# Attention loop on one Trainium2 core: VectorE's rotation moved behind the maxima of each step, and the maxima's turning product widened to 128 columns

## The chip, the cores and the metric

One Trainium2 chip; the kernel runs on one of its cores. The metric is device time in microseconds (us) of one execution. Engines are named as the profile names them: PE is TensorE's matmul, PEld its weight load, DVE VectorE, ACT ScalarE, POOL GpSimd, SP the queue that issues transfers. L543 is line 543 of the kernel before.

## The reference, cut to what matters

The model has four layers over 2048 rows of 128 features; the change touches the first alone, a full attention with 16 heads of 64:

```python
qkv = x @ qkv_w + qkv_b                      # heads H=16, D=64
q, k = rope(q), rope(k)                      # (t0*cos - t1*sin, t1*cos + t0*sin) on even/odd pairs
attn = softmax(einsum('bhqd,bhkd->bhqk', q, k) / 8)
out = einsum('bhqk,bhkd->bhqd', attn, v)
y = out @ out_w + out_b
```

Three more layers follow (a local attention with its feed-forward part, a scan, a gated feed-forward part), each with a layer norm.

## The kernel before

`mha_heads` computes the attention. Numbers go through TensorE as pairs of float16 (a high part and the remainder, "lo"), so that products keep float32-like precision. The work is cut into 64 **turns** (16 heads by 4 chunks of 512 queries), each of 8 **steps**; a step takes 256 of the 2048 keys. There are 512 steps, and each engine has the loop over them written out by hand; semaphores join the engines. I write j for the step within a turn, e for the turn.

In step p (turn e, step j) the engines do this:

- **PE**: `scores(p)`, four products of 512 columns (L385, L386) into `p_s`; `maxima`, two products of 512 columns (L370), one for each half of `p_m`, for the step 12 ahead (LEAD_M); `weigh`, twice twelve products of 64 or 65 columns (L400, L402, L404) for the step three back (LAG), into `p_o`. The order in a step is scores, first maxima product, 12 of weigh, second maxima product, 12 of weigh; at j=2 the first twelve and the first maxima product stand ahead of the scores. Added to this, once in each turn: at j=0 three projection products of 512 columns for the turn six ahead (L330 to L332, into `p_a`), at j=6 `turn_max` (L375, one product, which turns the negated maxima of 128 partitions x 4 into rows of `p_a`), at j=7 `project_v` (twelve products of 64 columns).
- **ACT**: two exponentials of each score block, to `probs_hi` in float16 (L511) and `probs` in float32 (L514); at j=4 also `high` (L474), the float16 copy of the rotated q and k.
- **POOL**: `probs_lo` = `probs` - `probs_hi` (L306), one instruction in each step; once in every four turns, after j=3, `split_weights` for a later head (L266, L268).
- **DVE**: two maxima reductions in each step (L589), one for each half of `p_m`. A product of `maxima` waits until the reduction of the step before has emptied the same half. Around the reductions stand, once in each turn: `cross_sin` (L543), `cross_cos` (L549), `cross_first` (L554) and `cross_second` (L558), the rotation of q and k; `low` (L569), the float16 remainder; `normalise` (L610, L612); `negate_max` (L596); `max_rows` (L602), which reads what `turn_max` wrote; `high_v` and `low_v` (L574, L579).
- **SP**: twelve transfers in each turn that spread `hi` and `lo` to the tiles of q and k.

`turn_max(e+1)` waits for `negate_max` (m_done) and for `low` (lo_done), since it writes the bank that `low` reads. `project_v` waits for `max_rows`, and the projection of the next turn for `low_v`. `weigh(p)` waits for POOL's `lo_pool`, `scores(p)` for the exponentials of step p-2. The projection, rotation, `low` and `project_v` are made for the turn six ahead, so the last six turns don't have them; the loop's transfers run far ahead of their use.

Of the kernel before, what the change touches and what calls it, by code (L numbers as in the profile page):

```python
# [6 lines left out]
ALU = mybir.AluOpType  # L7
ACT = mybir.ActivationFunctionType
AX = mybir.AxisListType.X
F32 = mybir.dt.float32  # L10
F16 = mybir.dt.float16
I32 = mybir.dt.int32

P = 128
# [5 lines left out]
TPC = CH // P  # L20
# [84 lines left out]
TURNS = HEADS * QC  # L105
STEPS_A = TURNS * PAIRS_A


LAG = 3
# [3 lines left out]
LEAD_M = 12  # L113
# [9 lines left out]
def phase_mha(nc, x_sb, ident, a, ln, local_scope, late_scope):  # L123


    with Scope(nc, "a_") as sc:
        attn = sc.sb("attn", [P, NT, HEADS * HD])
        wo = sc.sb("wo", [P, HEADS * HD // P, D])
        mha_heads(nc, x_sb, ident, a, attn, wo)
        late = LateWeights(late_scope, a)  # L130
        local = LocalWeights(local_scope, late_scope, a)
        mha_out(nc, x_sb, ident, ln, attn, wo, local, late)
    return local, late


def chunk(c):
    return slice(c * CH, (c + 1) * CH)


def mha_heads(nc, x_sb, ident, a, attn, wo):  # L140

    IC = HEADS * HD // P
    with Scope(nc, "ah_") as sc:
# [15 lines left out]
        hi = sc.sb("hi", [P, 2, CH], F16)  # L159
        lo = sc.sb("lo", [P, 2, CH], F16)  # L160
        part = sc.sb("part_max", [P, TPC, 4])
        negm = sc.sb("neg_max", [P, TPC], F16)
        identh = sc.sb("ident_f16", [P, P], F16)
        pb = sc.sb("probs", [P, RP, 2, CH])
        ph = sc.sb("probs_hi", [P, RW, 2, CH], F16)
# [9 lines left out]
        p_a = sc.ps("p_a", [P, CH])  # L175
# [13 lines left out]
        LAST_G = TURNS - 1  # L189
# [21 lines left out]
        with nc.Block() as block:  # L211
# [100 lines left out]
            def _(pe):  # L312
                pe.wait_ge(ident_in, 16)
                for c in range(NCH):
# [3 lines left out]
                    for t in range(TPC):  # L318
                        mm = pe.transpose(p_m[:, c % 2, t * P:(t + 1) * P], x_sb[:, c * TPC + t, :], ident[:, :])
                    mm.then_inc(x_turned, 1)  # L320
                pe.wait_ge(consts, 1)

                def project(out, g, which, ready):
                    h, c = divmod(g, QC)
# [47 lines left out]

                def turn_max(e):
                    pe.wait_ge(m_done, e + 1)
                    pe.matmul(p_a[0:TPC, 0:P], negm[:, :], identh[:, :], start=True, stop=True).then_inc(m_turned, 1)  # L375

                def scores(p):
                    e, j = divmod(p, PAIRS_A)
# [35 lines left out]
                for c in range(IC):  # L414
                    mm = pe.matmul(p_a[:, 0:D], bv[:, c:c + 1].to_broadcast([P, P]), wo[:, c, :], start=(c == 0),
                                   stop=(c == IC - 1))
                mm.then_inc(bias_turned, 1)
                early_v(LEAD_G - 2)
                for q in range(PAIRS_A):
                    maxima(q)  # L420
                pe.wait_ge(bias_done, 1)
                turn_max(0)
                early_v(LEAD_G - 1)
                for q in range(PAIRS_A, LEAD_M):
# [5 lines left out]
                for p in range(STEPS_A):  # L430
                    e, j = divmod(p, PAIRS_A)
                    g = e + LEAD_G
# [87 lines left out]
            def _(dve):  # L520
# [16 lines left out]
                def cross_sin(g):  # L537
                    h = g // QC
                    dve.wait_ge(proj_ready, g + 1)
                    dve.wait_ge(r_done, g)  # L540
                    if g > LEAD_G:
                        dve.wait_ge(first_half, g - LEAD_G)
                    dve.scalar_tensor_tensor(rot[:, :], p_a[:, :], bqk[:, 2, h:h + 1], sin[:, chunk(g % QC)], ALU.add,  # L543
                                             ALU.mult).then_inc(rot_done, 1)

                def cross_cos(g):
                    h = g // QC
                    dve.wait_ge(rot_done, g + 1)
                    dve.scalar_tensor_tensor(p_a[:, :], p_a[:, :], bqk[:, 2, h:h + 1], cos[:, chunk(g % QC)], ALU.add,  # L549
                                             ALU.mult).then_inc(cos_done, 1)  # L550

                def cross_first(g):
                    dve.wait_ge(cos_done, g + 1)
                    dve.tensor_tensor(p_a[0:HD, :], p_a[0:HD, :], rot[HD:P, :], ALU.add).then_inc(first_half, 1)  # L554

                def cross_second(g):
                    dve.wait_ge(cos_done, g + 1)
                    dve.tensor_tensor(p_a[HD:P, :], p_a[HD:P, :], rot[0:HD, :], ALU.subtract).then_inc(r_done, 1)  # L558
# [6 lines left out]
                def low(g):  # L565
                    dve.wait_ge(hi_done, g + 1)
                    if g >= 2:
                        dve.wait_ge(spread[g % 2], spread_after(g // 2))
                    dve.tensor_tensor(lo[:, g % 2, :], proj_bank(g), hi[:, g % 2, :], ALU.subtract).then_inc(lo_done, 1)  # L569

                def high_v(g):
                    h, c = divmod(g, QC)
                    dve.wait_ge(v_ready, g + 1)
                    dve.tensor_copy(vh[:, h % SETS, c * TPC:(c + 1) * TPC, 0:HD], v_tiles(g)).then_inc(vh_done, 1)  # L574

                def low_v(g):
                    h, c = divmod(g, QC)
                    dve.wait_ge(vh_done, g + 1)
                    dve.tensor_tensor(vl[:, h % SETS, c * TPC:(c + 1) * TPC, :], v_tiles(g),  # L579
                                      vh[:, h % SETS, c * TPC:(c + 1) * TPC, 0:HD], ALU.subtract).then_inc(vl_done, 1)  # L580

                def reduce_max(q, halves=(0, 1)):
                    e, i = divmod(q, PAIRS_A)
                    t, half = divmod(i, 2)
                    if i == 0 and e >= 1 and 0 in halves:
                        dve.wait_ge(m_done, e)
                    for b in halves:
                        dve.wait_ge(m_ready, 2 * q + b + 1)
                        dve.tensor_reduce(part[:, t, 2 * half + b:2 * half + b + 1], p_m[:, b, :], AX,  # L589
                                          ALU.max).then_inc(maxed, 1)  # L590

                def negate_max(e):
                    dve.wait_ge(maxed, 2 * PAIRS_A * (e + 1))
                    if e >= 1:
                        dve.wait_ge(m_turned, e)
                    dve.tensor_reduce(negm[:, :], part[:, :, :], AX, ALU.max, negate=True).then_inc(m_done, 1)  # L596

                def max_rows(e):
                    n, c = divmod(e, QC)
                    dve.wait_ge(m_turned, e + 1)  # L600
                    rows = qb[0:TPC, n % SETS, chunk(c)].rearrange("r (t q) -> r t q", q=P)
                    dve.scalar_tensor_tensor(rows, p_a[0:TPC, 0:P].unsqueeze(1).to_broadcast([TPC, TPC, P]), EXP_SHIFT,  # L602
                                             ident[0:TPC, 0:TPC].unsqueeze(2).to_broadcast([TPC, TPC, P]), ALU.add,
                                             ALU.mult).then_inc(mrow_ready, 1)

                def normalise(e):
                    n, c = divmod(e, QC)
                    dve.wait_ge(o_ready, e + 1)
                    o = p_o[:, 0:TPC * VW].rearrange("p (t w) -> p t w", w=VW)
                    dve.reciprocal(rcp[:, :], o[:, :, HD]).then_inc(rcp_done, 1)  # L610
                    dve.wait_ge(rcp_done, e + 1)
                    dve.tensor_tensor(attn[:, c * TPC:(c + 1) * TPC, n * HD:(n + 1) * HD], o[:, :, 0:HD],  # L612
                                      rcp[:, :].unsqueeze(2).to_broadcast([P, TPC, HD]), ALU.mult).then_inc(o_free, 1)

                dve.wait_ge(ident_in, 16)
                dve.tensor_copy(identh[:, :], ident[:, :]).then_inc(consts, 1)
                for c in range(NCH):
                    dve.wait_ge(xh_ready, c + 1)
                    dve.tensor_tensor(xl[:, chunk(c)], p_m[:, c % 2, :], xh[:, chunk(c)],
                                      ALU.subtract).then_inc(xl_ready, 1)  # L620
# [21 lines left out]
                for p in range(STEPS_A):  # L642
                    e, j = divmod(p, PAIRS_A)
                    g = e + LEAD_G
                    if p + LEAD_M < STEPS_A:
                        reduce_max(p + LEAD_M, (0,))
                    if g <= LAST_G:
                        if j == 1:
                            cross_cos(g)
                        if j == 3:  # L650
                            cross_second(g)
                        if j == 5:
                            low(g)
                    if j == LAG - 1 and e >= 1:
                        normalise(e - 1)
                    if p + LEAD_M < STEPS_A:
                        reduce_max(p + LEAD_M, (1,))
                    if j == 3 and e + 1 < TURNS:
                        negate_max(e + 1)
                    if g <= LAST_G:  # L660
                        if j == 0:
                            cross_sin(g)
                        if j == 2:
                            cross_first(g)
                        if j == 7:
                            high_v(g)
                            low_v(g)
                    if j == 6 and e + 1 < TURNS:
                        max_rows(e + 1)
                normalise(TURNS - 1)  # L670


# [1734 lines left out]
```

## Time and profile before

| | |
|---|---|
| time, median of 3 runs | 1828.27 us (1826.53 to 1828.4) |
| profiled execution, its own time | 1826.56 us |
| its span (first to last instruction) | 1824.8 us |
| PE busy | 1701.7 us (93%) |
| DVE busy | 1462.3 us (80%) |
| ACT busy | 1429.3 us (78%) |
| POOL busy | 1427.8 us (78%) |
| mean granted clock of TensorE | 0.978 of full speed |

Busy times are unions of an engine's instructions; a 512-column product has 0.38 us in the records though the next one starts 0.215 us later, so PE's busy share hides small gaps, and start times are read instead. The attention loop runs from 56.6 us to about 1195 us; the granted clock is 1.00 from 60 us to the end of the loop.

### The profile page before, as it was taken

How to read it: one execution, taken by the hardware profiler on the slowest of the kernel's cores; microseconds unless marked ns; L12 is line 12 of the kernel's file. 1: busy time of each engine (PE TensorE's matmuls, PEld its weight loads, DVE VectorE, ACT ScalarE, POOL GpSimd, SP SyncE). 2: the span in 40 equal slices, each digit the busy share in tenths (PEclk: the TensorE clock that was granted, in tenths of full speed). 3: DMA queues.
4: the chain of work that ended last, by engine and by line, in shares of the span. 5: the costliest groups of instructions: out<-in, count | busy, mean ns of one | idle time of the engine just before them, and what ended most of it. 6: DMA issues, size and time to landing. Idle time of an engine off the chain costs nothing. (4 is left out here: it accounts for less than half of the span.)

```text
span 1824.8 us, 53957 instructions
## 1 busy us (share of the span) xinstructions
PE 1701.7 (93%) x22682; PEld 1080.8 (59%) x22682; DVE 1462.3 (80%) x2658; ACT 1429.3 (78%) x1795; POOL 1427.8 (78%) x851
## 2 busy tenths in 40 slices
PE   5999999999999999999999999986989999978997
PEld 2466666666666666666666666683556666653454
DVE  5888888888888888888888887445988888855785
ACT  2688888888888888888888889834898888853464
POOL 6799999999999999999999999973665566624122
PEclk9899999999999999999999999997999999989999
DMA  5001010101001010100101010050211111110000
GB/s 143 21 25 28 22 30 22 27 25 27 24 25 26 24 31 20 29 24 25 26 25 27 20 28 2 2 169 17 44 38 37 37 37 37 34 26 1 1 0 24
DMA packets 76648, 56.12 MB, mean 31 GB/s; under 512 B 34764, under 2 KB 69752, under 8 KB 76408
## 3 DMA queue, kind: packets, MB, share of 16 engines
q1 hardware_dynamic: 76408, 52.69, 11.2%
q8 instruction: 179, 2.93, 0.7%
q14 instruction: 61, 0.50, 0.1%
HBM read 13.76 MB, written 1.05 MB: 8 GB/s over the span
## 5 line engine op out<-in xcount | busy, mean ns | idle before, releaser
L306 POOL TENSOR_TENSOR ah_probs_lo<-ah_probs,ah_probs_hi 128x1024 f16<-128x1024 f32 x512 | 1074.3, 2134 | 60.0 <-ACT ah_probs L514 60.0
L589 DVE TENSOR_REDUCE ah_part_max<-ah_p_m 128x1 f32<-128x512 f32 x1024 | 673.2, 685 | 140.7 <-PE ah_p_m L370 128.4
L511 ACT ACTIVATE ah_probs_hi<-ah_p_s 128x1024 f16<-128x1024 f32 x512 | 538.2, 1051 | 146.2 <-PE ah_p_s L386 139.9
L514 ACT ACTIVATE ah_probs<-ah_p_s 128x1024 f32<-128x1024 f32 x512 | 540.6, 1056 | 0.0
L400 PE MATMUL ah_p_o<-ah_v_hi,ah_probs_hi 128*128 128x65 f16 x4096 | 470.1, 195 | 5.7 <-POOL ah_probs_lo L306 5.1
L402 PE MATMUL ah_p_o<-ah_v_lo,ah_probs_hi 128*128 128x64 f16 x4096 | 470.3, 193 | 0.0
L404 PE MATMUL ah_p_o<-ah_v_hi,ah_probs_lo 128*128 128x65 f16 x4096 | 470.1, 194 | 0.0
L402 PEld LDWEIGHTS ah_p_o<-ah_v_lo,ah_probs_hi 128*128 128x128 f16 x4096 | 378.0, 98 | 96.9
L400 PEld LDWEIGHTS ah_p_o<-ah_v_hi,ah_probs_hi 128*128 128x128 f16 x4096 | 383.1, 98 | 71.9 <-POOL ah_probs_lo L306 8.8
L370 PE MATMUL ah_p_m<-ah_k_hi_lo,ah_q_hi_twice 128*128 128x512 f16 x1024 | 393.8, 385 | 21.4 <-DVE ah_part_max L589 18.0
L385 PE MATMUL ah_p_s<-ah_q_hi_twice,ah_k_hi_lo 128*128 128x512 f16 x1024 | 388.9, 380 | 0.8 <-ACT ah_probs L514 0.4
L386 PE MATMUL ah_p_s<-ah_max_q_lo,ah_one_k_hi 128*128 128x512 f16 x1024 | 388.3, 379 | 0.0
L404 PEld LDWEIGHTS ah_p_o<-ah_v_hi,ah_probs_lo 128*128 128x128 f16 x4096 | 379.2, 97 | 0.0
L370 PEld LDWEIGHTS ah_p_m<-ah_k_hi_lo,ah_q_hi_twice 128*128 128x128 f16 x1024 | 100.1, 98 | 99.2 <-DVE ah_part_max L589 36.4
L385 PEld LDWEIGHTS ah_p_s<-ah_q_hi_twice,ah_k_hi_lo 128*128 128x128 f16 x1024 | 100.0, 98 | 70.3 <-ACT ah_probs L514 1.4
L386 PEld LDWEIGHTS ah_p_s<-ah_max_q_lo,ah_one_k_hi 128*128 128x128 f16 x1024 | 100.1, 98 | 68.6 <-issue 0.3
L1079 POOL TENSOR_TENSOR ba_rot_sum<-ba_rot_parts 128x512 f32<-128x512 f32 x64 | 80.2, 1273 | 61.6 <-DVE ba_rot_parts L1464 61.6
L1102 POOL TENSOR_TENSOR ba_qk<-ba_rot_sum,ba_rnorm 128x1024 f32<-128x1024 f32 x32 | 60.9, 1903 | 72.5 <-issue 71.8
L1464 DVE TENSOR_TENSOR ba_rot_parts<-ba_p_qk,bw_rot 128x1024 f32<-128x1024 f32 x64 | 75.5, 1217 | 33.4 <-ACT ba_sq L1365 33.0
L1094 POOL TENSOR_TENSOR ba_probs_lo<-ba_probs,ba_probs_hi 128x1024 f16<-128x1024 f32 x32 | 68.2, 2131 | 5.6 <-ACT ba_probs L1374 5.6
L1365 ACT ACTIVATE ba_sq<-ba_p_qk 128x512 f32<-128x512 f32 x64 | 37.4, 593 | 39.6 <-PE ba_p_qk L1119 38.5
L2050 POOL TENSOR_TENSOR t_o_norm<-t_centred,t_rstd 128x512 f32<-128x512 f32 x4 | 4.3, 1076 | 69.3 <-DVE t_rstd L2142 69.3
(317 smaller groups left out, 3085.9 us busy)
## 6 DMA issues: line engine op xcount, KB each, us to landing
ba_v_skew<-ba_v_own SPq DMA_DIRECT2D x64, 129.0 KB, 2.3
ah_q_hi_twice<-ah_hi SPq DMA_DIRECT2D x232, 32.0 KB, 1.9
ah_k_hi_lo<-ah_hi SPq DMA_DIRECT2D x116, 32.0 KB, 1.9
ah_one_k_hi<-ah_hi SPq DMA_DIRECT2D x116, 32.0 KB, 1.9
ah_k_hi_lo<-ah_lo SPq DMA_DIRECT2D x116, 32.0 KB, 1.9
ah_max_q_lo<-ah_lo SPq DMA_DIRECT2D x116, 32.0 KB, 1.9
bw_rot<-in_rot SPq DMA_DIRECT2D x4, 512.0 KB, 9.8
ao_wqkv<-in_wqkv SPq DMA_DIRECT2D x2, 768.0 KB, 6.9
```

Of the source, the lines that this page charges most:

```text
L306: pool.tensor_tensor(pl[:, p % RW, :, :], pb[:, p % RP, :, :], ph[:, p % RW, :, :], ALU.subtract).then_inc(lo_pool, 1)
L370: pe.matmul(p_m[:, b, :], qa[:, s, rows], ka[:, s, chunk(2 * half + b)], start=True, stop=True).then_inc(m_ready, 1)
L385: pe.matmul(p_s[:, p % 2, i, :], ka[:, s, ks], qa[:, s, chunk(c)], start=True, stop=False)
L386: mm = pe.matmul(p_s[:, p % 2, i, :], kb[:, s, ks], qb[:, s, chunk(c)], start=False, stop=True)
L400: pe.matmul(o, hi_i, vh[:, s, kt, :], start=(kt == 0 and i == 0), stop=False, skip_group_check=True)
L402: pe.matmul(o[:, 0:HD], hi_i, vl[:, s, kt, :], start=False, stop=False, skip_group_check=True)
L404: mm = pe.matmul(o, lo_i, vh[:, s, kt, :], start=False, stop=(kt == KT - 1), skip_group_check=True)
L511: act.activation(ph[:, p % RW, :, :], p_s[:, p % 2, :, :], ACT.Exp, scale=HD ** -0.5)
L514: act.activation(pb[:, p % RP, :, :], p_s[:, p % 2, :, :], ACT.Exp, scale=HD ** -0.5).then_inc(exp_done, 1)
L589: dve.tensor_reduce(part[:, t, 2 * half + b:2 * half + b + 1], p_m[:, b, :], AX, ALU.max).then_inc(maxed, 1)
L1079: pool.tensor_tensor(out[:, :, :, f, :], part[:, :, 0, :, f, :], part[:, :, 1, :, 1 - f, :], ALU.add).then_inc(t3_done, 1)
L1464: dve.tensor_tensor(t12[:, s, :, :].rearrange("p r (h d) -> p r h d", d=DH), x4.unsqueeze(1).to_broadcast([P, 2, HEADS_B, DH]), lw.tab[:, ...
```

## The change

Two things are changed.

1. VectorE's order. Before, at odd steps (`cross_cos` j=1, `cross_second` j=3, `low` j=5) one operation of the rotation stood between the two reductions of a step. Now every one stands behind the second reduction, and `cross_cos` follows `cross_sin` at j=0. `negate_max` (j=3) comes after `cross_second`. `max_rows` (j=6) moves the other way, from behind the second reduction to between the two; `normalise` (j=2) stays between them.
2. `turn_max`. The tile of negated maxima is widened from 4 to 128 columns; columns 4 to 127 are set to zero once, at the start, and the product uses all 128 as its weights and writes 128 rows of `p_a` in place of 4. The first four are read as before.

```diff
-        negm = sc.sb("neg_max", [P, TPC], F16)
+        negm = sc.sb("neg_max", [P, P], F16)
...
-                pe.wait_ge(consts, 1)
+                pe.wait_ge(consts, 2)
...
-                    pe.matmul(p_a[0:TPC, 0:P], negm[:, :], identh[:, :], start=True, stop=True).then_inc(m_turned, 1)
+                    pe.matmul(p_a[:, 0:P], negm[:, :], identh[:, :], start=True, stop=True).then_inc(m_turned, 1)
...
-                    dve.tensor_reduce(negm[:, :], part[:, :, :], AX, ALU.max, negate=True).then_inc(m_done, 1)
+                    dve.tensor_reduce(negm[:, 0:TPC], part[:, :, :], AX, ALU.max, negate=True).then_inc(m_done, 1)
...
+                dve.memset(negm[:, TPC:P], 0.0).then_inc(consts, 1)
...
                     if p + LEAD_M < STEPS_A:
                         reduce_max(p + LEAD_M, (0,))
+                    if j == LAG - 1 and e >= 1:
+                        normalise(e - 1)
+                    if j == 6 and e + 1 < TURNS:
+                        max_rows(e + 1)
+                    if p + LEAD_M < STEPS_A:
+                        reduce_max(p + LEAD_M, (1,))
                     if g <= LAST_G:
-                        if j == 1:
+                        if j == 0:
+                            cross_sin(g)
                             cross_cos(g)
+                        if j == 2:
+                            cross_first(g)
                         if j == 3:
                             cross_second(g)
                         if j == 5:
                             low(g)
-                    if j == LAG - 1 and e >= 1:
-                        normalise(e - 1)
-                    if p + LEAD_M < STEPS_A:
-                        reduce_max(p + LEAD_M, (1,))
-                    if j == 3 and e + 1 < TURNS:
-                        negate_max(e + 1)
-                    if g <= LAST_G:
-                        if j == 0:
-                            cross_sin(g)
-                        if j == 2:
-                            cross_first(g)
                         if j == 7:
                             high_v(g)
                             low_v(g)
-                    if j == 6 and e + 1 < TURNS:
-                        max_rows(e + 1)
+                    if j == 3 and e + 1 < TURNS:
+                        negate_max(e + 1)
```

The order of VectorE's instructions in one turn (the second of the loop), from `cross_sin` at j=0 to `negate_max` at j=3, before:

```order
L543 SCALAR_TENSOR_TENSOR ah_rot_sin<-ah_p_a,ah_bias_qk,ah_sin 128x512
L589 TENSOR_REDUCE ah_part_max<-ah_p_m 128x1
L549 SCALAR_TENSOR_TENSOR ah_p_a<-ah_p_a,ah_bias_qk,ah_cos 128x512
L589 TENSOR_REDUCE ah_part_max<-ah_p_m 128x1 x2
L610 RECIPROCAL ah_rcp<-ah_p_o 128x4
L612 TENSOR_TENSOR a_attn<-ah_p_o,ah_rcp 128x4x64
L589 TENSOR_REDUCE ah_part_max<-ah_p_m 128x1
L554 TENSOR_TENSOR ah_p_a<-ah_p_a,ah_rot_sin 64x512
L589 TENSOR_REDUCE ah_part_max<-ah_p_m 128x1
L558 TENSOR_TENSOR ah_p_a<-ah_p_a,ah_rot_sin 64x512
L589 TENSOR_REDUCE ah_part_max<-ah_p_m 128x1
L596 TENSOR_REDUCE ah_neg_max<-ah_part_max 128x4
```

The same place in the changed kernel:

```order
L543 SCALAR_TENSOR_TENSOR ah_rot_sin<-ah_p_a,ah_bias_qk,ah_sin 128x512
L549 SCALAR_TENSOR_TENSOR ah_p_a<-ah_p_a,ah_bias_qk,ah_cos 128x512
L589 TENSOR_REDUCE ah_part_max<-ah_p_m 128x1 x3
L610 RECIPROCAL ah_rcp<-ah_p_o 128x4
L612 TENSOR_TENSOR a_attn<-ah_p_o,ah_rcp 128x4x64
L589 TENSOR_REDUCE ah_part_max<-ah_p_m 128x1
L554 TENSOR_TENSOR ah_p_a<-ah_p_a,ah_rot_sin 64x512
L589 TENSOR_REDUCE ah_part_max<-ah_p_m 128x1 x2
L558 TENSOR_TENSOR ah_p_a<-ah_p_a,ah_rot_sin 64x512
L596 TENSOR_REDUCE ah_neg_max<-ah_part_max 128x4
```

L549 has gone ahead of the reductions of j=1, and L558 behind the second reduction of j=3. The rest of the same turn, j=4 to j=7, in the changed kernel:

```order
L589 TENSOR_REDUCE ah_part_max<-ah_p_m 128x1 x4
L569 TENSOR_TENSOR ah_lo<-ah_p_a,ah_hi 128x512
L589 TENSOR_REDUCE ah_part_max<-ah_p_m 128x1
L602 SCALAR_TENSOR_TENSOR ah_max_q_lo<-ah_p_a,g_ident 4x512
L589 TENSOR_REDUCE ah_part_max<-ah_p_m 128x1 x3
L574 CAST ah_v_hi<-ah_p_a 128x4x64
L579 TENSOR_TENSOR ah_v_lo<-ah_p_a,ah_v_hi 128x256
```

Before, L569 stood one reduction earlier and L602 one reduction later. On PE the order stays; at j=6 the turning product alone has another form:

```order
 L370 MATMUL ah_p_m<-ah_k_hi_lo,ah_q_hi_twice 128x512
-L375 MATMUL ah_p_a<-ah_ident_f,ah_neg_max 4x128
+L375 MATMUL ah_p_a<-ah_ident_f,ah_neg_max 128x128
 L400 MATMUL ah_p_o<-ah_v_hi,ah_probs_hi 128x65
```

It stands where it stood, between the second maxima product of j=6 and the twelve products of `weigh`.

## Rows read from the trace of the kernel before

**Rows 1.** Waits, 99.39 to 1098.23 us: engine, line, waited for, us, times, longest

```profile
PE ah_p_m L370 <- DVE ah_part_max L589: 14.4, 56, 0.3
PEld ah_p_a L375 <- issue: 13.4, 56, 0.2
```

**Rows 2.** Timeline of PE, one turn's bounds, first score product at j=0

```profile
608.26 0.38 PE L385 MATMUL ah_p_s<-ah_q_hi_twice,ah_k_hi_lo 128*128 128x512 f16 x1
...
626.11 0.38 PE L385 MATMUL ah_p_s<-ah_q_hi_twice,ah_k_hi_lo 128*128 128x512 f16 x1
```

**Rows 3.** Timeline of PE at j=4: the two maxima products, weigh between them

```profile
617.85 0.38 PE L370 MATMUL ah_p_m<-ah_k_hi_lo,ah_q_hi_twice 128*128 128x512 f16 x1
618.07 0.19 PE L400 MATMUL ah_p_o<-ah_v_hi,ah_probs_hi 128*128 128x65 f16 x1
...
618.40 0.19 PE L404 MATMUL ah_p_o<-ah_v_hi,ah_probs_lo 128*128 128x65 f16 x1
618.85 0.39 PE L370 MATMUL ah_p_m<-ah_k_hi_lo,ah_q_hi_twice 128*128 128x512 f16 x1 [0.26 <-DVE ah_part_max L589]
```

**Rows 4.** Timeline of DVE, the same turn: start, duration, instruction, idle before

```profile
610.77 0.75 DVE L543 SCALAR_TENSOR_TENSOR ah_rot_sin<-ah_p_a,ah_bias_qk,ah_sin 128x512 f32<-128x512 f32 x1
...
612.93 0.76 DVE L549 SCALAR_TENSOR_TENSOR ah_p_a<-ah_p_a,ah_bias_qk,ah_cos 128x512 f32<-128x512 f32 x1
...
616.05 0.69 DVE L554 TENSOR_TENSOR ah_p_a<-ah_p_a,ah_rot_sin 64x512 f32<-64x512 f32 x1
616.66 0.67 DVE L589 TENSOR_REDUCE ah_part_max<-ah_p_m 128x1 f32<-128x512 f32 x1
617.36 0.71 DVE L558 TENSOR_TENSOR ah_p_a<-ah_p_a,ah_rot_sin 64x512 f32<-64x512 f32 x1
618.10 0.69 DVE L589 TENSOR_REDUCE ah_part_max<-ah_p_m 128x1 f32<-128x512 f32 x1
618.83 0.17 DVE L596 TENSOR_REDUCE ah_neg_max<-ah_part_max 128x4 f16<-128x16 f32 x1
...
620.72 0.69 DVE L589 TENSOR_REDUCE ah_part_max<-ah_p_m 128x1 f32<-128x512 f32 x1 [0.40 <-PE ah_p_m L370]
...
623.94 0.67 DVE L602 SCALAR_TENSOR_TENSOR ah_max_q_lo<-ah_p_a,g_ident 4x512 f16<-4x512 f32 x1
```

**Rows 5.** Timeline of PE, the first maxima product at j=5

```profile
620.30 0.38 PE L370 MATMUL ah_p_m<-ah_k_hi_lo,ah_q_hi_twice 128*128 128x512 f16 x1
```

**Rows 6.** Timeline of PE around the turning product at j=6

```profile
622.54 0.19 PE L400 MATMUL ah_p_o<-ah_v_hi,ah_probs_hi 128*128 128x65 f16 x1
...
622.90 0.38 PE L370 MATMUL ah_p_m<-ah_k_hi_lo,ah_q_hi_twice 128*128 128x512 f16 x1
623.21 0.22 PE L375 MATMUL ah_p_a<-ah_ident_f,ah_neg_max 128*4 128x128 f16 x1
623.36 0.20 PE L400 MATMUL ah_p_o<-ah_v_hi,ah_probs_hi 128*128 128x65 f16 x1
```

**Rows 7.** Groups by line, 80 to 1180 us: busy, mean ns, idle before

```profile
L370 PEld LDWEIGHTS ah_p_m<-ah_k_hi_lo,ah_q_hi_twice 128*128 128x128 f16 x978 | 95.6, 98 | 79.3 <-DVE ah_part_max L589 21.5
...
L375 PEld LDWEIGHTS ah_p_a<-ah_ident_f,ah_neg_max 128*4 128x4 f16 x62 | 5.0, 80 | 14.6 <-issue 14.6
```

**Rows 8.** Timeline of POOL: a plain turn, one with split_weights, the last turns

```profile
616.96 14.66 POOL L306 TENSOR_TENSOR ah_probs_lo<-ah_probs,ah_probs_hi 128x1024 f16<-128x1024 f32 x7 [0.83 <-ACT ah_probs L514]
...
652.66 4.22 POOL L306 TENSOR_TENSOR ah_probs_lo<-ah_probs,ah_probs_hi 128x1024 f16<-128x1024 f32 x2 [0.83 <-ACT ah_probs L514]
...
657.76 12.58 POOL L306 TENSOR_TENSOR ah_probs_lo<-ah_probs,ah_probs_hi 128x1024 f16<-128x1024 f32 x6
...
1081.03 16.77 POOL L306 TENSOR_TENSOR ah_probs_lo<-ah_probs,ah_probs_hi 128x1024 f16<-128x1024 f32 x8 [0.83 <-ACT ah_probs L514]
1098.23 96.12 POOL L306 TENSOR_TENSOR ah_probs_lo<-ah_probs,ah_probs_hi 128x1024 f16<-128x1024 f32 x46 [0.43 <-ACT ah_probs L514]
```

**Rows 9.** Timeline of ACT, the float16 copy of the rotated q and k

```profile
620.38 0.66 ACT L474 ACTIVATE ah_hi<-ah_p_a 128x512 f16<-128x512 f32 x1
```

## The prediction

> **What bounds the kernel now.** I read the granted clock first (1.00 all through the attention loop, so no term here hangs on it), then the waits in the steady loop, then the timelines of PE, DVE and POOL over one turn. The change touches only the loop of 512 steps. In it a turn lasts 626.11 - 608.26 = 17.85 us [rows 2], the same in every turn that I looked at. PE's products stand back to back nearly everywhere: a 512-column product takes 0.215 us of PE's time (617.85 to 618.07, [rows 3]), the twelve of `weigh` or of `project_v` 0.365 (622.54 to 622.90, [rows 6]). A turn has 51 of the first (32 scores, 16 maxima, 3 projections) and 17 of the second: 10.97 + 6.20 = 17.17 us. So about 0.65 us of each turn is not dense work, and it lies in two places.
>
> First, at j=4 PE has ended `weigh` at 618.07 + 0.365 = 618.43 but starts the second maxima product at 618.85: **0.42 us lost** [rows 3]. It waits for the half that j=3's second reduction empties, and that reduction (618.10 to 618.79) stood behind `cross_second`, 617.36 to 618.07 [rows 4]. PE starts 0.06 us after it ends. The waits show the same stop in each turn, 56 times in 56 turns; their 14.4 us are smaller than 56 x 0.42, because the recorded ends of `weigh`'s products cover part of the gap [rows 1]. The waits, then, undercount; starts don't.
>
> Second, around the turning product at j=6: the maxima product starts at 622.90, the turning product at 623.21, `weigh` at 623.36 [rows 6]. Dense, these would be 0.215 and, for 128 columns, 0.215 x 128/512 = 0.054. Measured 0.31 + 0.15 = 0.46 against 0.27: **0.19 us lost**. The load of 4 columns is not pulled ahead as the other loads are ("issue", 0.2 us, 56 times, [rows 1]), with nothing outstanding: `negate_max` ended at 619.00, `low` before 622.
>
> 0.42 + 0.19 = 0.61, and 17.85 - 0.61 = 17.24 agrees with 17.17 + 0.054. PE would be dense at 17.24 us.
>
> POOL is next. Seven of its instructions take 14.66 us [rows 8]; one lasts 2.13, so the pitch is 12.53/6 = 2.09 and a turn needs 16.71 us. A turn with `split_weights` needs 657.76 - 652.66 - 2 x 2.09 = 0.92 more [rows 8]. In the last 46 steps (no projections, no rotation) POOL is the bound: 96.12 us with no gap [rows 8]. Nothing of the change shortens these.
>
> **The change, part by part.** I count PE's time T from the first score product of a turn. With dense PE the maxima products start at T = 0.86, 1.44 (j=0), 3.53, 4.11 (j=1), 5.05, 6.49 (j=2), 7.57, 8.14 (j=3), 9.59, 10.17 (j=4), 11.61, 12.19 (j=5), 13.63, 14.21 (j=6), 15.71, 16.29 (j=7). A reduction can start 0.42 us after its product (620.30 to 620.72, [rows 5, 4]) and takes 0.69.
>
> *Sine and cosine back to back (j=0).* The last projection product starts at T 2.09, so sine runs 2.51 to 3.26, cosine 3.30 to 4.06 (durations 0.75 and 0.76, [rows 4]). j=1's first reduction, ready at 3.95, runs 4.1 to 4.8; PE wants it done for 5.05. Hidden by 0.25.
>
> *Rotation behind the second reduction (j=2, j=3).* j=2's second reduction runs 6.91 to 7.60, `cross_first` to 8.32 (0.69), j=3's reductions to 9.03 and 9.74, `cross_second` to 10.47 (0.71), `negate_max` to 10.66, j=4's reductions to 11.37 and 12.08. This counts durations end to end; the rows let a reduction start up to 0.08 before its predecessor's recorded end (616.66 against 616.05 + 0.69), so it is cautious. PE wants j=3's second at 10.17 (0.43 to spare, where before it came 0.42 late) and j=4's two at 11.61 and 12.19 (0.24 and 0.11 to spare). So the **0.42 us goes, and what is late next is nothing on DVE**: the three operations fit in the time of the four score products. `high` on ACT ran at 620.38, T = 12.1 [rows 9], long after `cross_second` even at its new end 10.47, so it is not delayed, nor are the transfers on SP that follow it.
>
> *`low` (j=5)* now ends about T 14.0 (j=5's second reduction starts 12.65, then 0.69 and 0.68); `turn_max` wants it at 14.43. Its four transfers leave some 0.7 us later, on data wanted a whole turn later.
>
> *`max_rows` between the reductions (j=6).* This adds a wait: in DVE's queue j=6's second reduction now stands behind `max_rows`, and that behind PE's turning product. The product starts at T 14.43; 0.22 (its record, [rows 6]) and 0.04 later DVE can go: 14.69 to 15.36 (0.67, [rows 4]), the reduction to 16.05. PE wants it at 16.29. Hidden by 0.2; DVE's idle time costs nothing. `project_v` waits less for `max_rows` than before.
>
> *128 columns.* The 0.19 us goes, if the width of the load is what holds it back. The price may lie anywhere from 0.27 us for the pair of products (all gained) to 0.46 (nothing gained); I take 0.27, since 128-column loads stand before every other product and none shows the gap. The load itself lasts 98 ns against 80 [rows 7], beside a running product. By the Trainium skill ("TensorE: Matmul & The Clock Gate", LDWEIGHTS) a load costs its columns divided by 1.2 per ns, an estimated 3 ns for 4 columns and 107 for 128; were that serial, the product would gain only 0.09 us a turn, and the sum would be 5.9 us worse. The row's 80 ns for 4 columns speaks against it. The memset at the start is one instruction of DVE, taken as nothing, since PE waits for later work of DVE.
>
> *POOL.* In plain turns its idle time shrinks from 17.85 - 16.71 = 1.14 to 0.53 us. In a `split_weights` turn it needs 17.63 against 17.24. Before, `weigh` of j=7, made by PE at j=2 of the next turn, starts at T 4.69, here 608.26 + 4.69 = 612.95. POOL began j=2 of the turn before at 616.96 - 17.85 = 599.11 [rows 8] and ended j=7 at 599.11 + 5 x 2.09 + 2.13 = 611.69, 1.26 us earlier. Now 1.26 - 0.61 - 0.92 = -0.27, and with 0.06 of release PE waits **0.33 us in each of the 14 such turns**: 4.7 us given back.
>
> *Sum.* Turn 0 has its own shape (less `weigh`, DVE busy throughout); I give it 0.4 of gain. Turns 1 to 56: 56 x 0.61 = 34.2. At the end POOL's queue takes over: it idles 0.43 us before its last 46 steps [rows 8], and that goes too, instead of 0.61 for turn 57. 0.4 + 34.2 + 0.4 - 4.7 = **30.3 us**. The profiled execution took 1826.56 us (span 1824.8 and 1.8 around it): 1796.3. The median of the runs shown lies 1.7 above it: 1798.0. I say 1797.
>
> **The rivals.** (A) The forecast above.
>
> (B) Only the product gains; the stop moves along DVE's queue instead of leaving (to j=1, where cosine ends 0.25 before it matters, or to j=4 and j=5, where 0.11 is left). Then 57 x 0.19 = 10.8 us, nothing given back by POOL: 1816. For it: spare times are small. Against it: four separate places have to be off by several tenths, and my durations are cautious.
>
> (C) Only the order gains: the 0.19 belongs to the product's waits on semaphores, not to its width. 57 x 0.42 = 23.9, POOL gives back 14 x 0.15: 1805. Against it: the projections wait for semaphores as well and leave no gap. The Trainium skill ("TensorEngine Tiling (Array Packing)", Key Properties) says that changing the tiling mode drains TensorE; by that, 4 columns are the cause and C is wrong, and the `128*4` in the product's row [rows 6] is such a mode.
>
> (D) Slower: `max_rows` holds up j=6's second reduction, so PE stops at j=7's second maxima product, the wait that takes the place of the one removed. It decides once the turned row reaches DVE more than 0.24 us after T 14.69, and the kernel is slower than before only from 0.24 + 0.61 = 0.85 on. At 1.0 us late: 57 x 0.15 = 8.6 more than 1827, 1836. It would take `low` ending beyond T 15.3, against 14.0.
>
> (E) The gain is met by POOL more harshly than I count: its plain turns run late too, and PE waits in each. With 16.71 + 0.92/4 = 16.94 us a turn on average it can't take back more than the 4.7 plus some coupling; twice that gives 1802. It lies in A's own range.
>
> **How the numbers follow.** A with E 0.80, B 0.06, C 0.09, D 0.03, and 0.02 that the two gains cancel against something to within 0.2% (3.7 us, about what a measurement of this kernel can tell from no change). Faster 0.95, same 0.02, slower 0.03. A's own range: 1792 (POOL gives back nothing) to 1802. The range goes from 1791.5 to 1805.5, which takes in C; B and D are left out.
>
> **What would show it.** The turn's period at 17.24 us, 17.6 in every fourth; PE's starts at j=4 0.365 apart from `weigh` to the maxima product; the pair of products at j=6 0.27 us long; no "issue" wait on L375; no wait of PE for the maxima; instead some 14 waits of `weigh` for POOL of about 0.3 us. I am wrong if waits for the maxima stay at about 56, or if PE waits for POOL in every turn.

## The result and the profile after

| | before | changed |
|---|---|---|
| median | 1827.72 us (4 runs) | 1796.15 us (4 runs, 1791.4 to 1797.96) |
| ratio | | 0.9824, 95% interval 0.9804 to 0.9844 |
| profiled execution, own time | 1826.56 us | 1796.48 us |
| its span | 1824.8 us | 1794.7 us |
| end of the attention loop (last POOL instruction) | 1194.35 us | 1163.42 us |

The prediction was 1797.0 us, range 1791.5 to 1805.5. By the last POOL instruction the loop ends 30.9 us earlier, where 30.3 had been worked out; outside it the profiled execution of the changed kernel was 0.8 us slower (the spans differ by 30.1).

The waits in the steady loop of the changed kernel, 99 to 1070 us (engine, line, waited for: us in total, times, longest); the rows of before are [rows 1]:

```profile
ACT ah_probs_hi L511 <- PE ah_p_s L386: 101.0, 111, 1.3
DVE ah_part_max L589 <- PE ah_p_m L370: 78.1, 283, 0.7
POOL ah_probs_lo L306 <- ACT ah_probs L514: 18.5, 42, 0.5
PEld ah_p_o L400 <- POOL ah_probs_lo L306: 8.1, 26, 0.4
```

PE's waits for a maxima reduction and the "issue" waits of L375, one of each in every turn before, have no row left. New is the last row, `weigh` waiting for POOL.

The timeline of PE around j=4 (start, duration, instruction), against [rows 3]:

```profile
618.82 0.38 PE L370 MATMUL ah_p_m<-ah_k_hi_lo,ah_q_hi_twice 128*128 128x512 f16 x1
619.03 0.19 PE L400 MATMUL ah_p_o<-ah_v_hi,ah_probs_hi 128*128 128x65 f16 x1
...
619.37 0.19 PE L404 MATMUL ah_p_o<-ah_v_hi,ah_probs_lo 128*128 128x65 f16 x1
619.39 0.38 PE L370 MATMUL ah_p_m<-ah_k_hi_lo,ah_q_hi_twice 128*128 128x512 f16 x1
```

From the start of the last product of `weigh` to the second maxima product it is 0.02 us, where it was 0.45. The same timeline around the turning product at j=6, against [rows 6]:

```profile
623.43 0.38 PE L370 MATMUL ah_p_m<-ah_k_hi_lo,ah_q_hi_twice 128*128 128x512 f16 x1
623.64 0.22 PE L375 MATMUL ah_p_a<-ah_ident_f,ah_neg_max 128*128 128x128 f16 x1
623.70 0.19 PE L400 MATMUL ah_p_o<-ah_v_hi,ah_probs_hi 128*128 128x65 f16 x1
...
625.50 0.38 PE L370 MATMUL ah_p_m<-ah_k_hi_lo,ah_q_hi_twice 128*128 128x512 f16 x1
```

The pair takes 623.70 - 623.43 = 0.27 us in place of 0.46.

The timeline of DVE in the same turn, from `cross_first` to the second reduction of j=6:

```profile
616.85 0.69 DVE L554 TENSOR_TENSOR ah_p_a<-ah_p_a,ah_rot_sin 64x512 f32<-64x512 f32 x1
617.46 1.27 DVE L589 TENSOR_REDUCE ah_part_max<-ah_p_m 128x1 f32<-128x512 f32 x2
618.76 0.71 DVE L558 TENSOR_TENSOR ah_p_a<-ah_p_a,ah_rot_sin 64x512 f32<-64x512 f32 x1
619.38 0.15 DVE L596 TENSOR_REDUCE ah_neg_max<-ah_part_max 128x4 f16<-128x16 f32 x1
619.57 1.29 DVE L589 TENSOR_REDUCE ah_part_max<-ah_p_m 128x1 f32<-128x512 f32 x2
...
622.46 0.68 DVE L569 TENSOR_TENSOR ah_lo<-ah_p_a,ah_hi 128x512 f16<-128x512 f32 x1
...
623.90 0.68 DVE L602 SCALAR_TENSOR_TENSOR ah_max_q_lo<-ah_p_a,g_ident 4x512 f16<-4x512 f32 x1
624.51 0.67 DVE L589 TENSOR_REDUCE ah_part_max<-ah_p_m 128x1 f32<-128x512 f32 x1
```

The turn starts at 618.82 - 9.59 = 609.23 (its first score product is recorded at 609.22). So `low` ends at T 13.91 (forecast "about 14.0"), `max_rows` begins at 14.67 (14.69), and the reduction behind it ends at 15.95 (16.05), 0.32 us before PE's product at 625.50.

The timeline of POOL over four turns, against [rows 8]:

```profile
565.91 4.22 POOL L306 TENSOR_TENSOR ah_probs_lo<-ah_probs,ah_probs_hi 128x1024 f16<-128x1024 f32 x2 [0.46 <-ACT ah_probs L514]
...
570.49 0.55 POOL L268 TENSOR_TENSOR ah_w_lo<-ah_w_head,ah_w_hi 128x192 f16<-128x192 f32 x1
571.00 29.29 POOL L306 TENSOR_TENSOR ah_probs_lo<-ah_probs,ah_probs_hi 128x1024 f16<-128x1024 f32 x14
...
617.93 16.77 POOL L306 TENSOR_TENSOR ah_probs_lo<-ah_probs,ah_probs_hi 128x1024 f16<-128x1024 f32 x8 [0.46 <-ACT ah_probs L514]
635.15 4.22 POOL L306 TENSOR_TENSOR ah_probs_lo<-ah_probs,ah_probs_hi 128x1024 f16<-128x1024 f32 x2 [0.45 <-ACT ah_probs L514]
...
1050.58 112.84 POOL L306 TENSOR_TENSOR ah_probs_lo<-ah_probs,ah_probs_hi 128x1024 f16<-128x1024 f32 x54 [0.45 <-ACT ah_probs L514]
```

A plain turn lasts 635.15 - 617.93 = 17.22 us (forecast 17.24, though the prediction's own count of dense work, 17.17 + 0.054, gives 17.22), four turns 635.15 - 565.91 = 69.24; one `split_weights` in four turns costs 69.24 - 4 x 17.22 = 0.36 us. After it POOL works through 14 instructions without a stop. At the end it is the bound for 54 steps, 46 before: it takes over one turn earlier.

### The profile page after: what moved, and what is told of

The parts are those of the page before. It is cut to its first block and busy times, and to the rows that moved or that the text cites. A ratio compares the mean times of both kernels' runs of the same rounds, so it can differ in the third digit from the quotient of the medians.

```text
span 1794.7 us, 53958 instructions
## 1 busy us (share of the span) xinstructions
PE 1685.9 (94%) x22682; PEld 1081.9 (60%) x22682; DVE 1456.9 (81%) x2659; ACT 1423.0 (79%) x1795; POOL 1425.9 (79%) x851
## 5 line engine op out<-in xcount | busy, mean ns | idle before, releaser
L511 ACT ACTIVATE ah_probs_hi<-ah_p_s 128x1024 f16<-128x1024 f32 x512 | 545.6, 1066 | 121.8 <-PE ah_p_s L386 120.1
L514 ACT ACTIVATE ah_probs<-ah_p_s 128x1024 f32<-128x1024 f32 x512 | 549.1, 1072 | 0.0
L400 PE MATMUL ah_p_o<-ah_v_hi,ah_probs_hi 128*128 128x65 f16 x4096 | 471.6, 194 | 8.2 <-POOL ah_probs_lo L306 6.3
L400 PEld LDWEIGHTS ah_p_o<-ah_v_hi,ah_probs_hi 128*128 128x128 f16 x4096 | 384.4, 98 | 83.0 <-POOL ah_probs_lo L306 18.5
```

Of the source, the lines that this page charges most:

```text
L400: pe.matmul(o, hi_i, vh[:, s, kt, :], start=(kt == 0 and i == 0), stop=False, skip_group_check=True)
L511: act.activation(ph[:, p % RW, :, :], p_s[:, p % 2, :, :], ACT.Exp, scale=HD ** -0.5)
L514: act.activation(pb[:, p % RP, :, :], p_s[:, p % 2, :, :], ACT.Exp, scale=HD ** -0.5).then_inc(exp_done, 1)
```

## The experiments

"Four turns" below is the time from one L268 (the second instruction of `split_weights`, under its number in that kernel) to the next in POOL's timeline; it repeats to a few hundredths of a us within an execution, and separates kernels more sharply than the total does. Before it is 71.39 us, changed 69.24. The runs were made in several sessions, and the kernel before had a median of 1825.13 us beside e1, e2, e3 and e8, not 1827.72; each ratio is to the kernel before of its own session. The last six rows are single executions, so there the four turns count, not the total.

| run | median, us | ratio to before (95%) | four turns, us |
|---|---|---|---|
| e1_order_only | 1806.36 | 0.9891 (0.9869 to 0.9913) | 69.84 |
| e2_width_only | 1816.01 | 0.9945 (0.9925 to 0.9965) | 70.61 |
| e3_j3_only | 1797.50 | 0.9841 (0.9821 to 0.9861) | 69.24 |
| e8_split_two_turns | 1791.75 | 0.9808 (0.9783 to 0.9833) | 68.88 |
| e4_width_32 | 1802.92, one run | | 69.87 |
| e4_width_64 | 1804.75, one run | | 69.92 |
| e4_width_96 | 1796.55, one run | | 69.24 |
| e7_turn_twice_4 | 1807.01, one run | | 70.00 |
| e10_rows_behind | 1795.66, one run | | 69.25 |
| e9_low_at_j6 | 1847.23, one run | | 72.81 |

### The two parts alone

```diff
 e1: the changed kernel, but
-pe.matmul(p_a[:, 0:P], negm[:, :], identh[:, :], ...)
+pe.matmul(p_a[0:TPC, 0:P], negm[:, 0:TPC], identh[:, :], ...)
```

> VectorE's new order alone, the turning product back at 4 columns. Theory (two independent losses of 0.42 and 0.19 us in each turn): a plain turn lasts 17.24 + 0.19 = 17.43 us, POOL gives back 0.15 us in each of 14 turns, the time is about 1806 us, and the wait before L375 is back, 0.2 us in each turn. Rival (the order alone does it, the width is worth nothing): 17.24 us a turn, 1797 us.

> 128 columns alone, VectorE's order as before. Theory: a turn lasts 17.85 - 0.19 = 17.66 us, PE still waits for VectorE before j=4's second maxima product (56 waits), POOL takes nothing back, 1817 us. Rival (PE's stop at j=4 swallows the time saved at j=6, since VectorE sets the turn): 17.85 us a turn, 1828 us.

e2 is the changed kernel with VectorE's loop taken from before. Both theories held. Order alone: a plain turn lasts 17.42 us (17.43 expected), so the 69.84 us for four turns are 4 x 17.42 and 0.16 of POOL's (0.15 expected); 1806.36 us against "about 1806". Its waits, less those of ACT, DVE and POOL, are

```profile
PEld ah_p_a L375 <- issue: 13.3, 56, 0.2
PEld ah_p_o L400 <- POOL ah_probs_lo L306: 2.5, 13, 0.2
```

The "issue" wait is back, and POOL holds `weigh` up once in each of 13 turns of the window, for at most 0.2 us. Width alone: 70.61 / 4 = 17.65 us a turn (17.66), 1816.01 us (1817), with PE's waits for the maxima as in [rows 1]:

```profile
PEld ah_p_m L370 <- DVE ah_part_max L589: 20.9, 55, 0.4
PE ah_p_m L370 <- DVE ah_part_max L589: 14.3, 55, 0.3
```

So the two losses are independent: 71.39 - 69.84 = 1.55 and 71.39 - 70.61 = 0.78 us in four turns sum to 2.33, of which the changed kernel shows 2.15. The missing 0.18 is POOL's, to 0.02: it takes 0.36 us back when both are there, 0.16 with the order alone and nothing with the width alone. In plain turns the parts add up: 17.85 to 17.42 and 17.85 to 17.65 are 0.43 and 0.20, and 17.85 to 17.22 is 0.63. Measured by the loop's end, the order alone gained 21.0 us (rival C's sum for it was 23.9 - 14 x 0.15 = 21.8), the width alone 11.9 (rival B's sum 10.8). Their sums were right to 1.1 us, their premises, that the changed kernel would gain one part only, were not.

### Which of the moves counts

```diff
 e3: 128 columns, VectorE's loop of before, but at j=3
-reduce half 0, cross_second, reduce half 1, negate_max
+reduce half 0, reduce half 1, cross_second, negate_max
```

> 128 columns, and of the new order only cross_second and negate_max behind j=3's second reduction; sine and cosine, cross_first, low and max_rows stand as before. Theory (only j=3 held PE up, the other moves are neutral): 17.24 us a turn, 1797 us. Rival (the moves work as a whole: with cosine at j=1 or low at j=5 between the reductions another stop shows once the first is gone): above 17.3 us a turn, with waits of PE for the maxima at j=2 or j=6, 1800 us or more.

```diff
 e10: the changed kernel, but at j=6
-reduce half 0, max_rows, reduce half 1
+reduce half 0, reduce half 1, max_rows
```

> The changed kernel with max_rows back behind j=6's second reduction. Theory (its wait on the turning product is hidden by 0.3 us): no change, 17.22 us a turn, 1796 us. Rival (the wait costs PE something at j=7, or a later max_rows delays project_v): a turn differs by more than 0.05 us.

Both are at the changed kernel's period, 69.24 and 69.25. All of the order's gain comes from one move, `cross_second` at j=3; the back-to-back sine and cosine, the later `low` and the earlier `max_rows` are neutral, as the prediction had it, which costed each at nothing.

### The slower side, made on purpose

```diff
 e9: the changed kernel, but
-                        if j == 5:
-                            low(g)
...
+                    if j == 6 and g <= LAST_G:
+                        low(g)
                     if j == 6 and e + 1 < TURNS:
                         max_rows(e + 1)
```

> The changed kernel with low moved from j=5 to j=6, between the first reduction and max_rows: the slower side of the prediction, made on purpose. Theory (the turning product waits for low, PE's queue stands behind it, and the maxima stay hidden): low ends at T 15.4 in place of 13.9, the product starts at 15.42 in place of 14.42, each turn lasts 1.0 us more, 18.2 us; POOL gives nothing back any more; 57 x 1.0 - 5 = 52 us, 1848 us. Rival (the product's wait is covered by PE's queue or by the following steps catching up): less than 0.5 us a turn, under 1825 us.

1847.23 us against 1848 expected, 72.81 / 4 = 18.20 us a turn. The timeline of PE at j=6 in this kernel:

```profile
706.42 0.38 PE L370 MATMUL ah_p_m<-ah_k_hi_lo,ah_q_hi_twice 128*128 128x512 f16 x1
707.61 0.23 PE L375 MATMUL ah_p_a<-ah_ident_f,ah_neg_max 128*128 128x128 f16 x1 [0.81 <-DVE ah_lo L569]
```

and of DVE:

```profile
706.26 0.69 DVE L589 TENSOR_REDUCE ah_part_max<-ah_p_m 128x1 f32<-128x512 f32 x1 [0.73 <-PE ah_p_m L370]
706.87 0.68 DVE L569 TENSOR_TENSOR ah_lo<-ah_p_a,ah_hi 128x512 f16<-128x512 f32 x1
707.88 0.68 DVE L602 SCALAR_TENSOR_TENSOR ah_max_q_lo<-ah_p_a,g_ident 4x512 f16<-4x512 f32 x1 [0.33 <-PE ah_p_a L375]
```

The product starts 1.19 us after the maxima product in place of 0.21; nothing catches up. One operation, behind one reduction more on an engine with idle time to spare, costs 51 us. It is a neighbour of rival D: the stop is at the turning product itself, and the steady loop has no wait of PE for the maxima in this kernel either, so D's own stop, at j=7's second maxima product, was not produced by any run. The changed kernel has time to spare before both: there `low` ends at T 13.91, and the product starts at 14.42.

### Why 4 columns cost 0.19 us

```diff
 e4, with N = 32, 64, 96: the changed kernel, but
-pe.matmul(p_a[:, 0:P], negm[:, :], identh[:, :], ...)
+pe.matmul(p_a[0:N, 0:P], negm[:, 0:N], identh[:, :], ...)
 e7: 4 columns, and the product made twice in a row
```

> The changed kernel with 32 columns in the turning product. Theory M (a product narrower than the full array sets it to another tiling, which has to be emptied on the way in and out): the pair of products at j=6 takes 0.46 us, the turn 17.43. Theory F (only loads of all 128 columns are fast and pulled ahead): the same. Theory P (the gap is that of a nearly empty load and shrinks with columns): about 0.42 us for the pair.

> 64 columns. Theory M: half the array is a tiling of its own, so 0.46 us for the pair. Theory F: 0.46 us as well. Theory P: about half the gap, 0.37 us.

> 96 columns. This tells M from F: M (96 columns need the full array, no switch): 0.27 us for the pair and a turn of 17.24 us. F (not all 128 columns, a slow load): 0.40 us or more for the pair. P: about 0.32 us.

> The changed kernel's order, with the 4-column product made twice in a row with the same result. M (the loss is the switch there and back): the second product adds about 0.06 us to the 0.46, a turn of 17.49 us. F or any cost of the narrow load itself: it adds 0.15 to 0.25 us, a turn of 17.6 us.

The timelines of PE and of its weight loads (PEld), with 64 columns:

```profile
715.00 0.38 PE L370 MATMUL ah_p_m<-ah_k_hi_lo,ah_q_hi_twice 128*128 128x512 f16 x1
715.31 0.11 PEld L375 LDWEIGHTS ah_p_a<-ah_ident_f,ah_neg_max 128*64 128x64 f16 x1 [0.24 <-issue]
715.31 0.24 PE L375 MATMUL ah_p_a<-ah_ident_f,ah_neg_max 128*64 128x128 f16 x1
715.48 0.10 PEld L400 LDWEIGHTS ah_p_o<-ah_v_hi,ah_probs_hi 128*128 128x128 f16 x1
715.49 0.20 PE L400 MATMUL ah_p_o<-ah_v_hi,ah_probs_hi 128*128 128x65 f16 x1
```

with 96:

```profile
709.41 0.38 PE L370 MATMUL ah_p_m<-ah_k_hi_lo,ah_q_hi_twice 128*128 128x512 f16 x1
709.41 0.12 PEld L375 LDWEIGHTS ah_p_a<-ah_ident_f,ah_neg_max 128*96 128x96 f16 x1
709.63 0.22 PE L375 MATMUL ah_p_a<-ah_ident_f,ah_neg_max 128*96 128x128 f16 x1
709.68 0.19 PE L400 MATMUL ah_p_o<-ah_v_hi,ah_probs_hi 128*128 128x65 f16 x1
```

and with the 4-column product made twice:

```profile
716.62 0.38 PE L370 MATMUL ah_p_m<-ah_k_hi_lo,ah_q_hi_twice 128*128 128x512 f16 x1
716.93 0.22 PE L375 MATMUL ah_p_a<-ah_ident_f,ah_neg_max 128*4 128x128 f16 x1
716.93 0.08 PEld L376 LDWEIGHTS ah_p_a<-ah_ident_f,ah_neg_max 128*4 128x4 f16 x1
716.98 0.22 PE L376 MATMUL ah_p_a<-ah_ident_f,ah_neg_max 128*4 128x128 f16 x1
717.13 0.20 PE L401 MATMUL ah_p_o<-ah_v_hi,ah_probs_hi 128*128 128x65 f16 x1
```

The pair takes 0.47 us with 32 columns, 0.49 with 64 and 0.27 with 96. The gap doesn't shrink with more columns, it is gone at 96, so theory P falls. F falls by the 96 columns as well: their load is not as fast as one of 128 (121 against 96 ns, rows at the end), and yet it is pulled ahead and costs nothing. M stands: the second narrow product adds 0.05 us (17.47 us a plain turn against the 17.42 of e1), what a dense one costs; the 0.09 us ahead and 0.10 behind are paid once for a stay in the narrow form, going in and coming out.

The rows of PEld show where the time goes. The 96-column load starts together with the full product ahead of it (709.41), so it is over when its own product may start. The 64-column load starts only at 715.31, 0.31 us after the full product, and its own product starts with it. The product doesn't wait for the load's recorded end; what comes late is the load's start. The full load behind it, of L400, is held as well, to 715.48. Between the two narrow products of e7 there is no such hold: the second load starts with the first product (716.93). So loads are pulled ahead from full to full and from narrow to narrow, and not from one form to the other.

The Trainium skill ("TensorEngine Tiling (Array Packing)", Key Properties) says that a change of the tiling mode drains TensorE, and the page lists modes of 64 and 32 columns and none of 96. If a product takes the smallest mode that holds its columns, 4, 32 and 64 change the mode and 96 doesn't, which agrees with the four widths measured. (The `128*4` in the row of before is the number of columns and not itself such a mode, as the prediction had it.) That the array is emptied during the hold is the page's statement; the rows show only the held loads. Where between 64 and 96 columns the border lies, and whether the columns of the weights or the partitions written set it, which are the same number here, was not tried.

### A version that beats both

```diff
 e8: POOL's split_weights in two functions, called at j=3
-split_weights(h)   # float16 copy and remainder, at turn 4h-7
+split_high(h)      # float16 copy, at turn 4h-8
+split_low(h)       # remainder, at turn 4h-7
```

> The changed kernel with POOL's split_weights cut in two: the float16 copy (0.42 us) one turn earlier, the remainder (0.51 us) where it was. Theory (the 0.36 us that PE loses in every fourth turn is POOL's 0.92 us coming in one piece, of which the spare time takes up some 0.6): both pieces fit, every turn lasts 17.22 us, no wait of weigh for POOL, 14 x 0.36 = 5 us less than the changed kernel, 1791 us. Rival (POOL is short of time on average, so that cutting its work moves the wait and keeps its sum): 1796 us, with about twice as many, smaller waits.

Four turns take 68.88 us, 17.22 each, and the waits in the steady loop, 99 to 1070 us, have no row of PE or PEld left; those that are left begin with these two (the lines of PE, ACT and DVE are numbered 7 higher in this kernel):

```profile
ACT ah_probs_hi L518 <- PE ah_p_s L393: 97.3, 111, 1.1
DVE ah_part_max L596 <- PE ah_p_m L377: 75.9, 286, 0.7
```

To compare it with the changed kernel under the same conditions, both ran once more on one chip:

> The changed kernel once more, beside the next run on the same chip, for a comparison of the two: 1796 us, 69.24 us for four turns.

> The version with split_weights cut over two turns, once more. Theory: 68.88 us for four turns against 69.24, 5 us less than the changed kernel on the same chip. Rival (its lower time came from the chip or from outside the loop): the two medians agree within 2 us.

1789.75 us (five runs, 1788.23 to 1794.21) against 1794.02 (four, 1793.18 to 1795.1): 4.3 us less, ratios to before 0.9795 (0.9775 to 0.9816) and 0.982 (0.98 to 0.984). Those intervals overlap; the loop settles it, which ended 4.4 us earlier (1046.24 + 112.82 against 1050.69 + 112.80 us in POOL's timelines: last stretch, start and length). The rival, that POOL was short of time on average, falls: `weigh`'s waits for it vanish, they don't spread.

## Why the prediction was right

**The 0.42 us at j=4.** Right, in size and in cause: with the order alone a plain turn is 0.43 us shorter, and the 1.55 us in four turns are 4 x 0.43 less POOL's 0.16, to 0.01. e3 adds what the prediction only argued, that the other moves are neutral.

**The 0.19 us at j=6.** Right in size, 0.78 / 4 = 0.195 from the width alone; the cause was named only in part. The premise ("if the width of the load is what holds it back") was right about the width, but it is not the load itself: at 96 columns it is not loaded as 128 are (121 against 96 ns) and no time is lost. What costs is the change to a narrow form and back. The weighed estimate of a serial load, 5.9 us worse, did not come: the 128-column load hides beside the product ahead of it. It was made from 3 ns for 4 columns and 107 for 128, where the records have 80 and 96.

**The terms costed at nothing.** Cosine was to end at T 4.06 and `max_rows` to start at 14.69; the latter began at 14.67. The spare times of j=4's reductions were called cautious and were: the reductions of j=4 ended at 620.86, T 11.63, where 12.08 had been counted, so 0.56 us were to spare, not 0.11.

**POOL's share.** Right: 0.33 us in each of 14 turns was forecast, 0.36 measured. The one thing not foreseen is that it comes in two pieces, 26 waits in 13 turns. Worked out from the same rows, `weigh` of j=4 (made at j=7) has next to no time to spare either once POOL is 0.92 us late. In the changed kernel's timeline of PE that is 0.06 us before `weigh` at j=7, and the larger piece before `weigh` at j=2 of the next turn:

```profile
648.38 0.20 PE L404 MATMUL ah_p_o<-ah_v_hi,ah_probs_lo 128*128 128x65 f16 x1
648.70 0.20 PE L400 MATMUL ah_p_o<-ah_v_hi,ah_probs_hi 128*128 128x65 f16 x1
```

These two of PE's products start 0.32 us apart, where 0.03 is the rule: 0.29 us lost.

**The sum.** 30.3 us forecast, 30.9 in the loop. The step that was a little off is the size of the plain turn: it is 0.63 us shorter, not 0.61, which makes 56 x 0.02 = 1.1 us more; POOL's 0.03 more in 14 turns takes 0.4 back. That leaves 0.1 for the start and the takeover at the end, the two rough terms. The 0.63 could have been had from the prediction's count of dense work, 17.85 - 17.22. That the total came within 1 us is in part luck: outside the loop the profiled execution lost 0.8 us that was not forecast, the executions of the changed kernel spread over 6.6 us, and of the 1.7 us added to come from the profiled execution to the median, which gave 1798.0, one was taken off for 1797 with no reason given.

**The rivals.** B and C each gave the right sum for a kernel with half of the change, and the wrong one for this kernel. D needed a turned row 0.85 us late to make it slower; it was 0.02 early. E's harsher form did not occur: all plain turns last 17.22 us.

## What to carry to other kernels

When an engine is dense, read the start times of its instructions over one period and compare them with a count of instructions by pitch: the two holes were 0.42 and 0.19 us in 17.85 and together worth 1.7%, and PE's busy share of 93% pointed at neither. On a helper engine, what matters is not how much it works but what stands ahead of the operation that the dense engine waits for; keep the rest in the time in which that engine does something else. A narrow product (64 columns or fewer here) between full ones is dearer than a full one, and a lump of work on the next tightest engine (0.92 us here) is better cut into pieces that fit its idle time.

## What the runs showed of the hardware

The load's record grows with its columns and then falls: 80 ns at 4 columns before [rows 7], and here the rows of L375 with 32, 64 and 96 columns and with 128 (median in the middle):

```profile
L375 PEld LDWEIGHTS ah_p_a<-ah_ident_f,ah_neg_max x64: 92/92/102, 49.0 to 1147.9; 128*32 128x32 f16 x64
```

```profile
L375 PEld LDWEIGHTS ah_p_a<-ah_ident_f,ah_neg_max x64: 106/106/128, 48.3 to 1147.6; 128*64 128x64 f16 x64
```

```profile
L375 PEld LDWEIGHTS ah_p_a<-ah_ident_f,ah_neg_max x64: 121/121/155, 48.6 to 1138.5; 128*96 128x96 f16 x64
```

```profile
L375 PEld LDWEIGHTS ah_p_a<-ah_ident_f,ah_neg_max x64: 95/96/103, 49.1 to 1139.0; 128*128 128x128 f16 x64
```

That is 14 to 15 ns for 32 columns, and 25 ns less at 128 than at 96. For full loads none of it is on the path: 96 and 128 columns both give 69.24 us for four turns. For narrow ones it may be: from the narrow product's start to that of the next product it takes 0.15, 0.16 and 0.18 us with 4, 32 and 64 columns, and four turns take 69.84, 69.87 and 69.92. Why, no run tells.

Executions of one kernel differ by 2 to 9 us. In the two profiled ones of the changed kernel the loop ended at 1163.42 and 1163.49 us while the spans were 1794.7 and 1791.9, so there the difference lies behind the loop. Here is the stretch from the loop's end to the kernel's end, first in f1_changed_again and then in f2_split_again (window, its length, PE's busy time and products, mean granted clock, then the share and GB/s of DMA):

```profile
1163.00:1791.00 628.00, 552.34 (x6272) 0.95 0.14 36
```

```profile
1159.00:1792.00 633.00, 555.15 (x6272) 0.94 0.14 36
```

The same 6272 products are spread over 5 us more (PE's busy time grows by 2.8), and the mean clock beside them is 0.94 instead of 0.95; whether the clock is all of it wasn't tried. In these two profiled executions that hides the whole gain of the loop (spans 1791.9 and 1792.4), which is why the loop's end was read and not the span.
